# One block for attention and experts: splits under the scatters, rows in three pieces, own banks for the last routing

## What is computed

```python
h = take(weight, x)
h = h + attention(layernorm(h))
xf = layernorm(h).reshape(N, D)
scores = softmax(xf @ wg);  top1 = argmax(scores)
rank = cumsum(one_hot(top1))[top1] - 1;  valid = rank < capacity
slot = where(valid, top1 * capacity + rank, trash)
buf = zeros(E * capacity + 1, D).at[slot].set(xf)
hid = gelu(buf @ W1 + b1);  y = hid @ W2 + b2
out = h + where(valid, y[slot], 0) * scores[top1]
```

## Time and profile before

| | us |
|---|---|
| three plain runs: median (lowest to highest) | 629.72 (628.26 to 635.33) |
| the profiled execution | 628.89 |
| its span, first to last instruction | 627.2 |
| TensorE matmul busy | 557.2 (89%) |
| TensorE weight load busy | 497.8 (79%) |
| VectorE busy | 418.6 (67%) |
| ScalarE busy | 348.1 (56%) |
| GpSimd busy | 258.4 (41%) |
| mean granted TensorE clock | 0.947 |

### The profile page before, as it was taken

The page is one execution under the profiler, slowest core; times in us unless marked ns, Lnnn a source line. Parts: engine busy times, 40 slices in busy tenths (PEclk is TensorE's granted clock), DMA queues, the critical chain, the costliest instruction groups (busy, mean ns, idle before and its releaser), DMA issues. The chain is left out here.

```text
span 627.2 us, 14064 instructions
## 1 busy us (share of the span) xinstructions
PE 557.2 (89%) x5179; PEld 497.8 (79%) x5234; DVE 418.6 (67%) x1073; ACT 348.1 (56%) x708; POOL 258.4 (41%) x316
## 2 busy tenths in 40 slices
PE   3678999999999999999976079999999999999993
PEld 3666777777778877777655069999999999999993
DVE  6356679988888988887664256565656565656521
ACT  2225555555655555564441248585858585858550
POOL 5447677765555566655552100404040404040403
PEclk9779999999999999999995569999999999999998
DMA  4698777656667655445111222151515151511101
GB/s 123 168 287 289 252 221 242 203 161 215 193 219 231 185 187 163 148 133 161 52 45 43 78 83 87 31 182 37 180 35 179 33 178 32 179 36 45 33 2 31
DMA packets 42580, 84.37 MB, mean 135 GB/s; under 512 B 6822, under 2 KB 32987, under 8 KB 38864
## 3 DMA queue, kind: packets, MB, share of 16 engines
q1 hardware_dynamic: 35600, 70.66, 35.2%
q0 software_dynamic: 6144, 12.67, 6.4%
q10 hardware_dynamic: 768, 0.13, 0.1%
HBM read 52.64 MB, written 31.74 MB: 135 GB/s over the span
## 5 line engine op out<-in xcount | busy, mean ns | idle before, releaser
L993 POOL DMA_INDIRECT out_dram<-ys,xs x48 | 51.0, 1063 | 221.2 <-DVE ys L1183 211.7
L400 POOL TENSOR_SCALAR_AFFINE_SELECT pt<-pt 128x512 f32<-128x512 f32 x128 | 81.3, 637 | 78.9 <-ACT pt L442 78.0
L442 ACT ACTIVATE pt<-C 128x512 f32<-128x512 f32 x128 | 76.4, 597 | 64.3 <-PE C L604 63.7
L1196 DVE TENSOR_TENSOR hl<-gl,hh 128x324 fp32r<-128x324 f32 x128 | 63.3, 495 | 37.5 <-ACT hh L1033 36.7
L781 DVE TENSOR_REDUCE mx<-S 128x4 f32<-128x512 f32 x128 | 86.5, 680 | 2.7 <-PE S L590 2.4
L590 PE MATMUL S<-ks,qs 96*128 96x128 bf16 x512 | 50.3, 220 | 10.5 <-issue 6.4
L1033 ACT ACTIVATE hh<-gl 128x324 fp32r<-128x324 f32 x128 | 58.6, 464 | 0.0
L701 PE MATMUL PV<-pt,va 128*32 128x128 f32 x1024 | 54.1, 285 | 0.9 <-ACT os L449 0.8
L590 PEld LDWEIGHTS S<-ks,qs 96*128 96x128 bf16 x512 | 40.2, 98 | 15.7 <-issue 0.8
L604 PE MATMUL C<-qs,ks 97*128 97x128 bf16 x512 | 49.8, 219 | 0.0
L1183 DVE SCALAR_TENSOR_TENSOR ys<-C,xs 108x256 f32<-108x256 f32 x48 | 21.8, 481 | 40.1 <-PE C L1083 40.1
(11 more groups left out here) (151 smaller groups left out, 1677.3 us busy)
## 6 DMA issues: line engine op xcount, KB each, us to landing
w_raw<-in_L_ffn_W_dram SPq DMA_DIRECT2D x16, 1024.0 KB, 8.6
qs<-q_parts SPq DMA_DIRECT2D x48, 256.0 KB
ks<-k_parts SPq DMA_DIRECT2D x48, 256.0 KB, 5.1
q_parts<-qp SPq DMA_DIRECT2D x16, 384.0 KB, 2.4
k_parts<-kp SPq DMA_DIRECT2D x16, 384.0 KB, 2.5
rows_of_slots<-w_raw SPq DMA_DIRECT2D x6, 877.5 KB, 8.7
xs<-rows_of_slots SPq DMA_DIRECT2D x8, 658.1 KB
out_dram<-h SPq DMA_DIRECT2D x16, 256.0 KB, 5.4
```

The source lines that it names most:

```text
L400: pool.affine_select(out=buf[:, :, :], in_=buf[:, :, :], compare_op=ALU.is_ge, fill=0.0, base=0, pattern=[[0, 4], [1, S]], channel_multipl ...
L442: act.activation(pt[u % 4][:, :, :], bC[u % 2][:, :].rearrange("p (j t) -> p j t", j=4), ACT.Exp, scale=SCALE).then_inc(a_exp, 1)
L993: pool.indirect_dma_start(out=outf, out_offset=bass.IndirectOffsetOnAxis(ap=xs[e.slot][:, j, D + 3:D + 4].bitcast(U32), axis=0), in_=ys[j] ...
L1196: dve.tensor_tensor(hl[:, f, cols], gl[u % 4][:, :], hh[:, f, cols].bitcast(F32), ALU.subtract).then_inc(v_hl, 1)
```

## The change

Four things are changed.

1. The two phases give back their streams as functions, and one block runs first the one and then the other on each engine. There is no barrier and no drain between them. What the barrier guarded is guarded by semaphores: SyncE waits for the stores and the scatters and then loads rows; ScalarE waits for the last slot numbers (`v_pos`) before it splits weights into memory that attention used. Tiles are declared in another order, so that `h` and `pos`, which the scatters still read, lie under the hidden tiles `hh` and `hl`, and not under tiles that are written first.
2. For expert 0, VectorE has all 8 splits first, and ahead of the first subtraction it normalises four row tiles.
3. Expert 0's rows come in three loads of two row tiles each, with a semaphore each.
4. The last group's transposes go to bank C0 and its logits to C1, which the scores no longer need; its normalisation and its transposes move ahead of group 14's routing and ranks.

```diff
-        attention_phase(nc, sb_in, sem, locals())
-        expert_phase(nc, sb_in, sem, locals())
+        routing = attention_phase(nc, sb_in, sem, locals())
+        experts = expert_phase(nc, sb_in, sem, locals())
+
+        block = whole.enter_context(nc.Block())
+
+        @block.sync
+        def _(sp):
+            routing["sync"](sp)
+            experts["sync"](sp)
...
+        def final(g):
+            return g.off == NG - 1
+
+        def turn_bank(g):
+            return bC[0] if final(g) else bM2
+
+        def logit_bank(g):
+            return bC[1] if final(g) else bM2
...
             steps(sp, step)
-            for i in range(2):
-                sp.wait_ge(d_slot[i], 16 * NG)
-            sp.wait_ge(d_rows, 16 * NG)
...
                 if g5:
-                    from_bank(x2t, bM2, pe_x2T, g5, a_x2t)
+                    if final(g5):
+                        wait(act, pe_lg, g5.times(1))
+                    from_bank(x2t, turn_bank(g5), pe_x2T, g5, a_x2t)
...
-                    if g and s == 5:
+                    if g and s == 5 and not final(g):
...
+                    g = group(n, i - 4)
+                    if g and s == 7 and final(g):
+                        wait(pe, v_xn2, g.times(1, 1))
+                        wait(pe, a_exp, UNITS * NG)
+                        turn4(turn_bank(g), xn2).then_inc(pe_x2T, 1)
...
-                if not g4:
+                if not g4 and g5 and not final(g5):
                     second_norm(g5)
...
                 maxima(7)
+                if g4 and final(g4):
+                    wait(dve, pe_x2T, g4.times(1))
+                    second_norm(g4)
                 if g5:
                     route(g5)
...
-            load_rows(expert(0, 0))
+            sp.wait_ge(d_rows, 16 * NG)
+            for i in range(2):
+                sp.wait_ge(d_slot[i], 16 * NG)
+            rows_of = slots[0:SL, :].rearrange("(p j) c -> p j c", j=NT)
+            for r in range(TURNS):
+                sp.dma_start(xs[0][:, 2 * r:2 * r + 2, :], rows_of[:, 2 * r:2 * r + 2, :]).then_inc(d_first[r], 16)
             load_rows(expert(0, 1))
-
-            sp.wait_ge(d_xs[0], 16)
...
+            act.wait_ge(v_pos, NG)
             e0 = expert(0, 0)
             for c in range(PIECES):
                 split(e0, c)
...
-                wait(dve, d_xs[e.slot], e.round(16, 16))
+                if e.off == 0:
+                    dve.wait_ge(d_first[j // 2], 16)
+                wait(dve, d_xs[e.slot], e.round(16, 16) if e.slot else e.round(16))
...
             e0 = expert(0, 0)
-            for c in range(PIECES // 2):
+            for c in range(PIECES):
                 split(e0, c)
-            normalise(e0, 0)
-            normalise(e0, 1)
-            normalise(e0, 2)
+            for j in range(4):
+                normalise(e0, j)
             turned(e0, 0)
-            normalise(e0, 3)
-            turned(e0, 1)
             normalise(e0, 4)
             normalise(e0, 5)
-            split(e0, 4)
+            turned(e0, 1)
             turned(e0, 2)
-            for c in (5, 6, 7):
-                split(e0, c)
```

More of the change, by code:

```diff
@@ L124, in lm_block @@
         d_raw = [sem(f"d_raw{q}") for q in range(2)]
+        d_rows, d_slot, v_pos = sem("d_rows"), [sem(f"d_slot{i}") for i in range(2)], sem("v_pos")
         def load_w1(eng, e, q):
@@ L136, in lm_block, with _ @@
         load_half = (load_w1, load_w2)
-        attention_phase(nc, sb_in, sem, locals())
-        expert_phase(nc, sb_in, sem, locals())
+        routing = attention_phase(nc, sb_in, sem, locals())
[5 more added lines that the diff above has]
+            experts["sync"](sp)
+        @block.gpsimd
+        def _(pool):
+            routing["gpsimd"](pool)
+            experts["gpsimd"](pool)
+        @block.scalar
+        def _(act):
+            routing["scalar"](act)
+            experts["scalar"](act)
+        @block.tensor
+        def _(pe):
+            routing["tensor"](pe)
+            experts["tensor"](pe)
+        @block.vector
+        def _(dve):
+            routing["vector"](dve)
+            experts["vector"](dve)
 def attention_phase(nc, sb_in, sem, v):
@@ L159, in attention_phase @@
         sb = sb_in(scope)
+        h = sb("h", [P, NB, ROW], F32)
+        pos = [sb(f"pos{i}", [P, GB], U32) for i in range(2)]
         identb = sb("identb", [P, P], BF16)
@@ L229, in attention_phase @@
         d_sh = [sem(f"d_sh{i}") for i in range(RING)]
-        d_rows, d_slot = sem("d_rows"), [sem(f"d_slot{i}") for i in range(2)]
+        d_rows, d_slot, v_pos = v["d_rows"], v["d_slot"], v["v_pos"]
         g_set, g_cst, v_cst = sem("g_set"), sem("g_cst"), sem("v_cst")
@@ L243, in attention_phase @@
             sem("v_" + n) for n in ("h1", "st2", "mv2", "ve2", "xn2", "lmax", "leq", "first", "dl", "se", "w"))
-        v_oh, v_cn, v_over, v_pl, v_pm, v_base, v_pos = (
-            sem("v_" + n) for n in ("oh", "cn", "over", "pl", "pm", "base", "pos"))
+        v_oh, v_cn, v_over, v_pl, v_pm, v_base = (
+            sem("v_" + n) for n in ("oh", "cn", "over", "pl", "pm", "base"))
         p_q3, p_k3, p_sel, p_rs1, p_rs2 = (sem("p_" + n) for n in ("q3", "k3", "sel", "rs1", "rs2"))
@@ L277, in weight_columns, with sync @@
                     for k in range(KC) for c in range(KC)]
-        block = scope.enter_context(nc.Block())
-        @block.sync
-        def _(sp):
+        def sync(sp):
             sp.dma_start(xi[:, :], x).then_inc(d_x, 16)
@@ L337, in _, with gpsimd @@
             steps(sp, step)
-            for i in range(2):
-                sp.wait_ge(d_slot[i], 16 * NG)
-            sp.wait_ge(d_rows, 16 * NG)
-        @block.gpsimd
-        def _(pool):
+        def gpsimd(pool):
             pool.memset(identf[:, :], 0.0).then_inc(g_cst, 1)
@@ L424, in _, with scalar @@
             steps(pool, step)
-        @block.scalar
-        def _(act):
+        def scalar(act):
             for m in range(4):
@@ L513, in _, with tensor @@
             steps(act, step)
-        @block.tensor
-        def _(pe):
+        def tensor(pe):
             def turn4(dst, src):
@@ L664, in step @@
                             for k in range(KC):
-                                last = pe.matmul(bM2[:, b * E:(b + 1) * E], x2t[:, k, b * S:(b + 1) * S],
+                                last = pe.matmul(logit_bank(g)[:, b * E:(b + 1) * E], x2t[:, k, b * S:(b + 1) * S],
                                                  wgs[:, k, :], start=(k == 0), stop=(k == KC - 1))
                         last.then_inc(pe_lg, 1)
+                    g = group(n, i - 4)
[3 more added lines that the diff above has]
+                        turn4(turn_bank(g), xn2).then_inc(pe_x2T, 1)
                     g = group(n, i - 6)
@@ L705, in _, with vector @@
             steps(pe, step)
-        @block.vector
-        def _(dve):
+        def vector(dve):
             dve.wait_ge(d_x, 16)
@@ L908, in _ @@
             steps(dve, step)
+        return {"sync": sync, "gpsimd": gpsimd, "scalar": scalar, "tensor": tensor, "vector": vector}
 def expert_phase(nc, sb_in, sem, v):
     D, E, KC, F, FC, SL, NT, TS, NH, N = (v[n] for n in ("D", "E", "KC", "F", "FC", "SL", "NT", "TS", "NH", "N"))
-    slots, outf = v["slots"], v["outf"]
+    slots, outf, d_rows, d_slot, v_pos, NG = (v[n] for n in ("slots", "outf", "d_rows", "d_slot", "v_pos", "NG"))
     bS, bC, bPV, bM0, bM1, bM2 = (v[n] for n in ("bS", "bC", "bPV", "bM0", "bM1", "bM2"))
@@ L941, in expert_phase @@
         d_xs = [sem(f"d_xs{q}") for q in range(2)]
+        d_first = [sem(f"d_first{r}") for r in range(TURNS)]
         d_out = [sem(f"d_out{j}") for j in range(NT)]
```

9 lines of the change are left out of this document (4 added, 5 removed).

## The result

| | before | changed |
|---|---|---|
| median of 11 runs each, us | 632.32 | 627.77 |
| lowest and highest | 628.26, 635.33 | 625.17, 630.01 |
| ratio to before, 95% interval | | 0.993 (0.9906 to 0.9953) |
| profiled execution | 628.89 | 630.01 |
| its span | 627.2 | 626.9 |

The change makes the kernel faster by 0.7%, some 4.5 us, where 8.7 us were forecast. Its time lies outside the range given. The two profiled spans are nearly the same, which at first looks as if nothing had been gained. They have to be read in four stretches, each between two events that both traces show: the end of group 15's variance (line 747 before, 782 after), the first expert matmul, the end of GpSimd's last store instruction, and the end of the span.

A forecast was written before the change was run, and what follows sets the result against it. It took TensorE to bound the expert loop and changed the stretch before it: 2.1 - 0.4 + 3.8 + 2.0 + 1.2 = 8.7 us gained, 628.89 - 8.7 = 620.2 us, range 617.8 to 623.5.

The forecast's parts named there:

- step 3: Between the scatters' landing and the row load's issue: without the block end, 3.88 us shrink to 0.1, 3.8 gained.
- a rival was built on it: At the row load: what kept GpSimd busy until 356.07 might hold the load too; gain 4.9, 624.0 us, chance 0.05.
- Step 1: Last group's routing: own banks and earlier normalisation bring slot numbers at 345.57, not 347.65; 2.1 us gained.
- Step 2: Last scatters beside expert 0's splits on VectorE: 0 to 0.6 us lost together, taken as 0.4.
- The rival of a whole split for each: Each last scatter waits for one whole split, 2 x 0.68 instead of 0.4; gain 7.7, 621.2 us, chance 0.06.
- starvation: GpSimd's last scatters get in only when VectorE's splits stop, at 351.2; gain 4.4, 624.5 us, chance 0.06.
- Step 4: Expert 0's row load in pieces: first piece lands after 2.8 us (bounds 2.2 and 4.83), not 4.83; 2.0 gained.
- Step 5: Expert 0's normalise, transpose, round and subtract ladder: reordered, it takes 4.4 us instead of 5.6; 1.2 gained.
- The base: The time before the change from which gains were subtracted: the profiled execution, 628.89 us.
- The signs named: Trace events foretold from routing to expert loop, such as slot numbers at 345.6 and first expert matmul at 358.1.
- the prediction's own price: TensorE's clock early in the expert loop: each us at the low level costs 0.46.
- the test of the loop: From first expert matmul to the end: the forecast is wrong if this exceeds 260.4 us by over 1.5.

The follow-up runs named there:

- the repeat: The changed kernel run again unaltered as a control; median 628.83 us beside 631.74 for the kernel before, ratio 0.9945.

## Why the prediction was wrong

The forecast gain was 8.7, the border's gain in the profiles 7.8, and what reached the end of the span 4.8.

**The step that failed is step 3, in its last sentence:** "GpSimd's own tail to 356.07 stays, but its next work is the first expert's output". The drain does not stay; it is removed there, and the one at the end has to do its work. The row was in view, 7.165 us of a drain that outlived the last scatter's landing by 3.6, and a rival was built on it, but only as something that might hold the load. The question that was not put is what the drain works on, and who does that later. The runs answer the second half: with the attention phase's 64 transfers left to it, the drain at the end holds the end of the span for 3.1 more (7.32 for 4.25), and with a drain behind the routing the tail is back at 4.23. What it works on for them they do not show. The removal itself gave 3.81, from 3.88 to 0.07, as forecast; net 0.7 of it is left.

**Step 1** was right in mechanism and size: 1.96 for 2.1 in the two profiles. With the banks undone it was 1.07, in an execution whose clock was high there.

**Step 2** had the right sign and was mis-sized. From slot numbers to landing 5.88 where it was 4.80: 1.1 lost and not 0.4; the repeat and the variants have 0.7 to 0.9. The row it went by, 0.2 for one meeting, was of a scatter that met a pair of splits near their end: the pair is over at 430.19, 0.33 after the scatter's start, so it had not met two splits in full. Against splits back to back it was 0.40 and 0.52 on the instructions. The rival of a whole split for each, 2 x 0.68, lies above all of these and the forecast below, the first profile nearer the rival; starvation did not come. What the Trainium skill says (SBUF — State Buffer, Who interferes with whom), that a VectorE instruction with two SBUF inputs contends with a GpSimd instruction that reads SBUF, the traces confirm: 1.38 and 1.50 with the splits, 0.98 without. That the later one waits for a whole instruction of 0.68 they do not show.

**Step 4** gave 1.74 for 2.0 (3.09 and not 2.8), and the undone pieces show two parts: 2.3 or more for the pieces, and 0.5 that one load would lose here against before, perhaps by the earlier reload. The bounds held.

**Step 5** gave 1.4 for 1.2, and undoing the order alone took back 1.4. Two normalisations that overlap make 0.64 where 0.75 was taken.

**The base.** 628.89 for the profiled execution was at the low end of what the kernel before does: the medians beside the four sets of runs are 632.32, 631.74, 628.62 and 630.94. So of the 7.6 between 620.2 and 627.77, 3.4 are the base, 3.1 the drain and 0.9 the border, which makes 7.4. The base alone would have put the forecast at 623.6, at the upper end of the range; the gain is half of the forecast because of the drain.

**The signs named.** This execution was 4.5 late before any changed instruction, so the places are compared with that taken off. The slot numbers came as told (8.01 behind the variance), the load 0.07 behind the landing as told, and the last 4.19 near the 4.4. Two signs did not: the scatters took 1.38 and 1.50 and not 1.0 to 1.3, and the first normalisation came 3.12 behind the issue and not 2.8. The first expert matmul was at 363.44 and not 358.1, of which 0.9 is the border. TensorE's clock rose 4.3 behind that matmul and not 6 (the windows below, with the columns of the windows above); by the prediction's own price that is 0.8 less, but the loop is the same to 0.03, and it lies anywhere between 254.9 and 256.7 in the 14 profiles.

```profile
367.50:367.75 0.25, 0.25 (x3) 0.25 (x2) 0.00 (x0) 0.25 (x1) 0.00 (x0) 0.50 1.06 356
367.75:368.00 0.25, 0.25 (x3) 0.25 (x2) 0.00 (x0) 0.25 (x1) 0.00 (x0) 0.80 0.86 283
```

Of the test of the loop, 260.4 from the first expert matmul to the end, the trace has 263.5: over by 3.1, and that was the sign for the failed step.

## What to carry to other kernels

A barrier's price is not the time between two events at its place. Ask of each engine's part what work it does, and whether another instruction has to do it once that part is gone: GpSimd's drain took the longer, the more indirect transfers had gone out since the last one. Put it where GpSimd is idle, or close the block without it when every transfer is waited for on its own semaphore. And compare two traces stretch by stretch between events that both have, since a run may lose before the change what it gains at the change.

## What was not expected of the hardware

A GpSimd drain at the kernel's end was over, behind the last indirect transfer's instruction, after 2.0 us with 6 such transfers since the last drain, 2.7 with 24, 4.0 with 48 and 7.1 with 112, though the last store had landed after 1.7 each time; elsewhere it was 5.3 with 64, 7.2 with 88 and 8.8 with 106. Two-input VectorE instructions back to back made a GpSimd scatter instruction 1.38 and 1.50 instead of 0.98. And the changed kernel and its variants, whose instructions differ only behind that point, finished the variance of their 16th group anywhere within 6 us (337.6 to 343.6); two executions of the very same program were 2.9 apart.
